# A graph layer on one core: histogram one-hots compared out of PSUM, and the row gathers issued without a pace

## The reference, cut to what matters

```
h    = relu(layernorm(x))
deg  = number of edges with row == node;  deg_inv = rsqrt(deg), 0 where deg is 0
norm = deg_inv[row] * deg_inv[col]
msg  = (sum over 4 bases b of comps[type, b] * h[col] @ bases[b]) * alpha[type] * norm
out  = x + segment_sum(msg, row)
```

## Time and profile before

| | |
|---|---|
| median of three runs | 767.62 us (767.0 to 768.07) |
| the profiled execution | 762.65 us |
| its span, first to last instruction | 760.8 us |
| mean granted TensorE clock | 0.938 of 2.4 GHz |
| busy: TensorE matmul, VectorE, ScalarE, GpSimd | 565.7, 595.4, 368.6, 548.0 us |
| instructions on GpSimd's queue that issue DMAs | 196 gathers, 196 scatters |

### The profile page before, as it was taken

One profiled execution on the slowest core, in us unless ns is written; L12 is line 12 of the kernel. 1 busy time (PEld: TensorE's weight loads), 2 busy tenths in 40 slices (PEclk: granted clock), 3 DMA queues, 4 the chain that ended last, 5 costly groups with the idle time before them and its releaser, 6 DMA issues. The chain is left out here.

```text
span 760.8 us, 13653 instructions
## 1 busy us (share of the span) xinstructions
PE 565.7 (74%) x3922; PEld 396.5 (52%) x3922; DVE 595.4 (78%) x2624; ACT 368.6 (48%) x1494; POOL 548.0 (72%) x404
## 2 busy tenths in 40 slices
PE   1999995566576886659769778777889669788860
PEld 0766654344354664446556556555666446554430
DVE  4999995578577897749879899869998869896630
ACT  0144346245343565455646565644566546465530
POOL 1788886344237777877888888888888778777875
PEclk9999997988798999999989999989999989999995
DMA  3899989989944545344444445435444534444332
GB/s 116 293 353 350 321 306 336 315 276 349 317 131 91 94 98 103 54 85 89 95 81 98 95 80 96 96 54 117 76 79 94 112 63 96 78 71 73 35 36 24
DMA packets 56527, 108.89 MB, mean 143 GB/s; under 512 B 9291, under 2 KB 48216, under 8 KB 55636
## 3 DMA queue, kind: packets, MB, share of 16 engines
q0 software_dynamic: 34496, 25.72, 25.0%
q1 hardware_dynamic: 5372, 55.14, 20.0%
q10 hardware_dynamic: 16584, 27.16, 11.6%
HBM read 94.89 MB, written 64.61 MB: 210 GB/s over the span
## 5 line engine op out<-in xcount | busy, mean ns | idle before, releaser
L389 POOL DMA_INDIRECT out_dram<-acc,scatter_idx x196 | 313.2, 1598 | 97.2 <-issue 43.7
L368 POOL DMA_INDIRECT rows<-in_x_dram,dst_i x196 | 232.8, 1188 | 107.5 <-issue 39.0
L723 PE MATMUL pst<-table_bits,turned_hot 128*128 128x198 f16 x1568 | 177.0, 261 | 79.4 <-DVE masked L476 63.4
L742 PE MATMUL pst<-bases_sb,h_turned 128*128 128x512 f32 x392 | 211.6, 623 | 0.0
L723 PEld LDWEIGHTS pst<-table_bits,turned_hot 128*128 128x128 f16 x1568 | 143.1, 103 | 106.4 <-issue 50.6
L513 DVE SCALAR_TENSOR_TENSOR part_sum<-pst,coef,part_sum 128x128 f32<-128x128 f32 x392 | 115.9, 344 | 104.7 <-ACT part_sum L636 100.2
L750 PEld LDWEIGHTS pst<-rows,same 128*128 128x128 f32 x392 | 71.3, 197 | 184.0 <-issue 160.5
L476 DVE SCALAR_TENSOR_TENSOR masked<-iota_h,lo,pst 128x198 f32<-128x198 f16 x392 | 141.7, 416 | 15.9 <-PE pst L723 8.7
L636 ACT ACTIVATE part_sum<-pst,coef 128x128 f32<-128x128 f32 x196 | 71.1, 363 | 154.2 <-PE pst L742 114.3
L750 PE MATMUL pst<-rows,same 128*128 128x128 f32 x392 | 83.5, 296 | 72.8 <-ACT acc L646 69.9
L646 ACT ACTIVATE acc<-pst,sum_scale 128x128 f32<-128x128 f32 x196 | 71.5, 365 | 81.9 <-DMA out_dram<-acc,scatter_idx 56.3
(11 more groups left out here) (71 smaller groups left out, 413.6 us busy)
## 6 DMA issues: line engine op xcount, KB each, us to landing
out_dram<-in_x_dram SPq DMA_DIRECT2D x50, 1000.0 KB
src_row<-src_rows ACTq DMA_DIRECT2D x25, 512.0 KB
edge_row<-edge_rows ACTq DMA_DIRECT2D x45, 256.0 KB
rows<-in_x_dram,dst_i POOLq DMA_INDIRECT x196
out_dram<-acc,scatter_idx POOLq DMA_INDIRECT x196
rows<-edge_rows ACTq DMA_DIRECT2D x10, 175.0 KB
edge_row<-edge_rows SPq DMA_DIRECT2D x4, 256.0 KB
src_row<-src_rows SPq DMA_DIRECT2D x2, 512.0 KB
```

What stands on the lines that cost most here:

```text
L368: pool.indirect_dma_start(row(t), None, x, bass.IndirectOffsetOnAxis(ap=dst_i[:, t:t + 1], axis=0)) \
L389: pool.indirect_dma_start(out, bass.IndirectOffsetOnAxis(ap=scatter_idx[:, t:t + 1], axis=0), acc[:, t % ACC_RING, :], None, compute_op=AL ...
L723: last = pe.matmul(pst[:, LOOK + t % 2, k * LO:(k + 1) * LO], turned_hot[:, g % 2, c, k * W + j * P:k * W + (j + 1) * P], table[:, c * LO: ...
L742: pe.matmul(pst[:, PRODUCT + t % 4, :], h_turned[:, g % 2, j, :], bases_sb[:].rearrange("d b f -> d (b f)"), start=True, stop=True).then_i ...
```

## The change

It makes a copy of the 512 numbers of `iota_h` in PSUM bank 1 (as 256 float32 words that hold two 16-bit numbers each), and both comparisons of the histogram read that copy. It takes away `pace` and the ring of eight semaphores, so that each group has its own semaphore. 148 gathers stand ahead of the first scatter in place of 88, and the other 48 come one with three scatters in place of seven with ten. The wait of gather 115 for the histogram's scratch stays.

```
-    GATHER_RING = 8
...
-    HIST_GATHERS, LOOK_GATHERS, FIRST_GATHERS = 56, 64, 88
+    FIRST_GATHERS = 148
...
     def gathers_until(t):
-        return min(TILES, FIRST_GATHERS + (7 * t + 9) // 10)
+        return min(TILES, FIRST_GATHERS + t // 3)
...
-        row_gathered = [sem(f"row_gathered{r}") for r in range(GATHER_RING)]
+        row_gathered = [sem(f"row_gathered{g}") for g in range(GROUPS)]
...
-            def pace(t):
-                if 0 < t < HIST_GATHERS:
-                    pool.wait_ge(hot_used, t * TILES // HIST_GATHERS)
-                elif HIST_GATHERS <= t < LOOK_GATHERS:
-                    pool.wait_ge(look_ps, (t - HIST_GATHERS + 1) * FIRST_LOOK * GROUP // (LOOK_GATHERS - HIST_GATHERS))
-                elif LOOK_GATHERS <= t < FIRST_GATHERS:
-                    pool.wait_ge(product_ready, (t - LOOK_GATHERS) // 2 + 1)
...
             def gather(t):
                 g = t // GROUP
-                if t % GROUP == 0 and g >= GATHER_RING:
-                    pool.wait_ge(row_squared, g - GATHER_RING + 1)
-                pace(t)
...
-                    .then_inc(row_gathered[g % GATHER_RING], 16)
+                    .then_inc(row_gathered[g], 16)
...
+            iota_ps = pst[:, LOOK + 1, 0:CHUNKS * P // 2]
+            dve.tensor_copy(iota_ps, iota_h[:].bitcast(F32))
+            iota_ps = iota_ps.bitcast(F16)
...
-                dve.tensor_scalar(hots[:, b, 0:CHUNKS * P], iota_h[:], src_hi[:, t:t + 1], None, ALU.is_equal)
-                dve.tensor_scalar(hots[:, b, CHUNKS * P:], iota_h[:, 0:LO], lo[:, 1, t:t + 1], None,
+                dve.tensor_scalar(hots[:, b, 0:CHUNKS * P], iota_ps, src_hi[:, t:t + 1], None, ALU.is_equal)
+                dve.tensor_scalar(hots[:, b, CHUNKS * P:], iota_ps[:, 0:LO], lo[:, 1, t:t + 1], None,
                                   ALU.is_equal).then_inc(hot_ready, 1)
...
             def stats(g):
-                act.wait_ge(row_gathered[g % GATHER_RING], 16 * GROUP * (g // GATHER_RING + 1))
+                act.wait_ge(row_gathered[g], 16 * GROUP)
```

## The result

| | median, us | range | ratio to the kernel before, 95% interval |
|---|---|---|---|
| kernel before, beside it (4 runs) | 767.31 | 764.4 to 768.07 | |
| changed kernel (4 runs) | 952.65 | 949.15 to 953.72 | 1.2416 [1.237, 1.2463] |
| its profiled execution | 952.01 | span 950.2, clock 0.839 | |

The forecast was 750, the range ended at 787. The change made the kernel 24% slower. One thing is needed to read what follows: the experiments ran on five chips of the same kind, numbered 14, 6, 8, 3 and 11, and for this change the chips differ. The number of the chip of this result isn't known; it behaves as chip 14. The ratio of each run is taken against the kernel before, run beside it.

A forecast was written before the change was run, and what follows sets the result against it. It took VectorE to bound the histogram and GpSimd's queue the main loop. Terms +35.5 - 2.7 - 4.3 - 0.7 - 45.7 = -17.9 us took the median from 767.6 to 749.7, say 750; range about 722 to 787.

The forecast's parts named there:

- the wait of gather 115 costs nothing: Histogram: 115 gathers end at 158 us, the histogram at 148, so gather 115's wait for it adds nothing.
- the rivals: Four: main loop held by VectorE and TensorE (0.16), comparison at 1.03 ns (0.09), PSUM free (0.07), gathers slow in histogram (0.08).
- Part 1: Histogram: comparisons reading PSUM run at half the rate, 0.50 ns a column, +35.5 us.
- Part 2's rate: Histogram: with the comparisons' form changed, gathers come 1.25 us apart from the start.
- Part 2, the copy: Start-up: 60 more gathers beside the copy of x delay its end by 12.5 us to 232, hidden before the first sum.
- Part 3: Start-up: TensorE's wait for ScalarE goes, -2.7 us; step 4 falls from 23.2 to 18.9 us, -4.3.
- Part 4, steps 5 to 11: Main loop: seven steps with two groups of statistics each, 13.7 us a step, 96 us in all, -0.7.
- Part 4, the 29 steps: Main loop to its end: 10.1 us a step instead of 11.68, 293 us in all, -45.7.
- the first rival: Main loop: VectorE and TensorE hold it about as much as GpSimd; no gain gives 796 us, half way 773; chance 0.16.
- Tail: After the main loop: unchanged at 95 us, since it has no gathers in either kernel.
- The sum without the standstill: Whole kernel: all terms together -17.9 us, profiled execution from 762.65 to 744.8 us.

The follow-up runs named there:

- e9: The changed kernel, same instructions with one empty line added to the text, on chip 3: 774.05 us, ratio 1.0156.
- e14: The changed kernel to the letter, on chip 14: 943.27 us, ratio 1.2348.
- e16: The changed kernel with two waited fills ahead of each of the first gathers, 1.6 us apart, on chip 14: 778.69 us, ratio 1.0193.
- e1: The kernel before with only both histogram comparisons reading the copy in PSUM, on chip 6: 791.23 us, ratio 1.0381.
- e2: The changed kernel with both comparisons back in SBUF, gathers still unpaced, on chip 6: 753.18 us, ratio 0.9892.
- e17: The kernel of e8, run on chip 14: 881.64 us, ratio 1.1513.
- e12: The kernel of e8 with 128 gathers ahead of the first scatter instead of 148, then four with nine scatters, on chip 3: 725.03 us, ratio 0.9517.
- e8: The kernel of e2 with at most one group of statistics a step instead of two, on chip 8: 723.38 us, ratio 0.9523.

## Why the prediction was wrong, point by point

- **Part 2, "the wait of gather 115 costs nothing" and, with it, that an unpaced run of gathers costs the other engines nothing: this step failed.** It was a term put at nothing without a reason. The gathers themselves came as forecast (1.25 us, 115 of them by 158; with VectorE at work, in e9, 1.31 us and the 148th over at 207.8 for 199). What I did not ask was what the other engines do meanwhile. They stood still, the histogram ended at 291 us in place of 148, and gather 115 waited 136 us for it. This cost some 179 us (the result against e9; 165 by e14 against e16, both on chip 14). None of the rivals had it, so the range missed it as well. What in the chip holds the engines is open. The rows that could have warned of it were the "remote" and "issue" waits at 112 to 130 us.
- **Part 1 held.** Distances of 0.39 and 0.23 us as forecast; the histogram ends at 145.7 (e9) for 148. A column costs (465 - 301) / 314 = 0.52 ns in the groups above, 0.50 forecast. The Trainium skill (VectorE: DVE Perf Modes, "Why PSUM operands drop a tier") allows a PSUM operand half the elements a cycle that 16 bits in SBUF get; the trace agrees. Its price on the kernel was 30 us alone (e1), and 21 with free gathers (e9 against e2, on two chips on which the kernel before takes the same), for in e2 the 148 gathers, not the histogram, set the first scatter at 238.
- **Part 2's rate held too.** Beside comparisons from PSUM gathers last 0.95 us, beside those from SBUF mostly 1.47 to 2.07 (e1, e2; the first eight in e2 only 0.95 to 1.15). The Trainium skill (SBUF — State Buffer, the "DVE blocks DMA" trap) says that a 2-port VectorE instruction keeps GpSimd from writing descriptors; the trace agrees, and only while VectorE runs (e17).
- **Part 2, the copy: mis-sized, without effect.** The copy was not held until 232 us by the 60 gathers more; in e9 no traffic is left from 218 to 224 us (0 GB/s), and in the kernel before, whose copy I had ended at the first scatter (219.7), none from 218 to 220. The sums come later, so nothing changed.
- **Part 3: the sum came out by luck.** In e9 the first step row after the start-up is at 234.9 (240 forecast), step 4 lasts 22.9 us (18.9): together step 5 at 257.7 for 258.9. Two errors cancel. The copy had ended long before step 4 and the step kept its length (23.2 before), so the copy's end was not what made it long.
- **Part 4, steps 5 to 11: mis-sized.** 111.0 us in e9 (257.7 to 368.8) for 96. Two groups of statistics cost 13.4 us only in steps 6 and 7 (280.7 to 307.6), then 14.8 to 15.8, and the first step of the seven takes 22.9. I had put a step at 13.7. Of the 15 us lost 9 are in the first step, whose length has another cause that was not isolated (it is 20 to 31 us with one group a step too, e12 and e8), and 6 in the other six. In the trace two groups stand in one piece ahead of what the others wait for.
- **Part 4, the 29 steps: mis-sized.** 309.5 us in e9 (10.67 each) for 293 (10.1): a gain of 29 of the 45.7. This is at the edge of the first rival, which I had let decide from 10.7 upwards and given 0.16: VectorE is busy 282.8 / 29 = 9.75 us of each step and GpSimd's queue has its 9.4, and I read it so that they do not fit into each other as closely as I took them. No run isolates it. What the runs show is that GpSimd's queue no longer sets the step: e12, where it needs 10.0 us a step, takes 10.7, and e8 10.6.
- **Tail: forecast unchanged at 95, 91 us in e9.**
- **The sum without the standstill:** forecast 744.8 for the profiled execution; -1 (step 5), +15, +16.5, -4 make 771; e9's was 770.89. So without the standstill the time would still have missed the forecast by 26 us, and the change would have cost 1.6% in place of giving 2.3%.

## What to carry to other kernels

A pace or a ring on a queue of indirect DMAs may also be what keeps the other engines alive: before taking it away, ask what a long unbroken run of gathers does to the engines beside it, look for small "issue" and "remote" waits where such a run already occurs, and time the result on more than one chip. Work that is done earlier is worth only what its successor in the queue can use: here the gathers came in time, and the statistics that they allowed pushed ScalarE's urgent work back by 6 us a step. One group a step and the comparisons left in SBUF gave 0.95, where the chip stood it.

## What the runs showed of the hardware that I had not expected

Back-to-back indirect gathers from GpSimd (0.95 us each, 0.30 between) held TensorE for long stretches to one matmul in 2 to 3.5 us, VectorE to 14 of 141 us busy and ScalarE to a wait of 145 us. They began to do so some nine gathers into the run, and let go of VectorE for good only 19 us after the last was issued. Chip 14 did so on both occasions, and chip 3 not at all (VectorE 140 of 141 us) with the same instructions and much the same traffic (334 and 343 GB/s). With two fills between them, 1.6 us apart, the effect was gone on chip 14 too; whether by the distance, the fills or the waits is not known. In the main loop, where a scatter stands between the gathers, the 29 steps take 309 us with and without it. The kernel before hardly tells such chips apart: 763.89 and 767.15 us on chip 14, 761.89 on chip 3.
